# Low-rank products of an RWKV-style block packed three to the array, decay's by token halves, and the pieces of a step in a new order

## The reference

```python
xa = ln(x);  sx = shifted(xa) - xa
xxx = tanh((xa + sx * maa_x) @ maa_w1)              # 512 -> 5 streams x 32
xxx = einsum('blfd,fde->blfe', xxx, maa_w2)         # each stream 32 -> 512
xm = xa + sx * (maa_stack + xxx)                    # xk, xw, xv, xr, xg
w = exp(-exp(time_decay + tanh(xw @ td_w1) @ td_w2))  # 512 -> 64 -> 512
r, k, v = xr @ Wr.T, xk @ Wk.T, xv @ Wv.T;  g = silu(xg @ Wg.T)
# per head (32 heads of 16): out = r . (u * k v^T + s);  s = k v^T + w * s, token by token
og = groupnorm(out);  x1 = x + (og * g) @ Wo.T
xc = ln(x1);  x = x1 + sigmoid(xr2 @ Wfr.T) * (relu(xk2 @ Wfk.T)**2 @ Wfv.T)
```

## Time and profile before

| | |
|---|---|
| median of 3 runs | 3876.71 us (3876.33 to 3880.83) |
| the profiled execution | 3876.33 us; its span 3874.6 us |
| busy in the span | PE 94%, DVE 72%, ACT 48%, POOL 3% |
| mean granted TensorE clock | 0.972 |
| chain that ended last | PE 85%, DVE 7%, issue 3%, ACT 3%, SP's queue 2%, DMA 1% |

### The profile page before, as it was taken

One profiled execution on the slowest core, in us unless ns is written; L12 is line 12 of the kernel. 1 busy time (PEld: TensorE's weight loads), 2 busy tenths in 40 slices (PEclk: granted clock), 3 DMA queues, 4 the chain that ended last, 5 costly groups with the idle time before them and its releaser, 6 DMA issues.

```text
span 3874.6 us, 80327 instructions
## 1 busy us (share of the span) xinstructions
PE 3644.6 (94%) x33648; PEld 2808.0 (72%) x33648; DVE 2770.9 (72%) x4009; ACT 1853.5 (48%) x2867; POOL 109.9 (3%) x204
## 2 busy tenths in 40 slices
PE   6899999999999999999999999966998998998898
PEld 4677777777777777777777777753785686686587
DVE  3788888878888888888878888742674665565465
ACT  1455555545555455555555555532453453354353
POOL 1000000000000000000000000000000000000000
PEclk9899999999999999999999999978999999999999
DMA  2122233322233222332233322213230240231221
GB/s 109 55 72 99 89 108 110 123 99 102 95 108 110 93 96 99 123 108 101 88 110 110 110 100 95 100 62 112 50 99 22 57 111 13 66 76 48 66 46 44
DMA packets 90229, 337.19 MB, mean 87 GB/s; under 512 B 16512, under 2 KB 37632, under 8 KB 63360
## 3 DMA queue, kind: packets, MB, share of 16 engines
q0 software_dynamic: 27648, 201.34, 14.6%
q1 hardware_dynamic: 62208, 130.52, 11.7%
HBM read 252.11 MB, written 16.78 MB: 69 GB/s over the span
## 4 chain that ended last, share of the span: by engine, by line
PE 85%; DVE 7%; issue 3%; ACT 3%; SPq 2%; DMA 1%; POOL 0%; ACTq 0%; DVEq 0%; POOLq 0%
PE psum L663 33%; PE psum L949 9%; PE psum L672 5%; PE psum L732 4%; PE psum L895 3%; PE psum L960 3%; PE psum L709 3%; PE psum L924 3%; PE psum L633 3%; PE psum L936 2%; DVE rw L1482 2%; PE psum L897 1%; PE psum L979 1%; DVE psum L1664 1%; PE psum L644 1%
## 5 line engine op out<-in xcount | busy, mean ns | idle before, releaser
L663 PE MATMUL psum<-rw 128*128 128x256 f32 x6144 | 1426.7, 388 | 12.1 <-DVE rw L1320 7.2
L663 PEld LDWEIGHTS psum<-rw 128*128 128x128 f32 x6144 | 1173.0, 194 | 244.9 <-issue 76.0
L949 PEld LDWEIGHTS psum<-mem 128*128 128x128 f32 x4096 | 490.5, 192 | 27.2 <-issue 12.1
L949 PE MATMUL psum<-mem 128*128 128x128 f32 x4096 | 503.1, 276 | 0.0
L1278 ACT ACTIVATE mem<-psum,mem 128x1024 f32<-128x1024 f32 x256 | 285.4, 1115 | 435.4 <-DVE mem L1667 435.4
L1482 DVE TENSOR_TENSOR rw<-rw 128x2048 f32<-128x2048 f32 x192 | 432.7, 2285 | 11.9 <-PE psum L732 11.1
L1664 DVE CUSTOM_DVE_ANT_0 psum<-psum,mem 128x1024 f32<-128x1024 f32 x256 | 314.9, 1230 | 8.2 <-PE psum L936 6.6
L1365 DVE SCALAR_TENSOR_TENSOR rw<-psum,rw 128x256 f32<-128x256 f32 x480 | 199.2, 477 | 150.2 <-PE psum L633 94.0
L1675 DVE COPY mem<-psum 128x512 f32<-128x512 f32 x256 | 177.1, 692 | 133.7 <-PE psum L949 133.6
L1068 ACT ACTIVATE rw<-psum 128x512 f32<-128x512 f32 x192 | 111.8, 595 | 325.5 <-PE psum L663 325.3
L1106 ACT ACTIVATE rw<-psum 128x512 f32<-128x512 f32 x192 | 202.2, 1138 | 130.9 <-PE psum L709 129.2
(11 more groups left out here) (144 smaller groups left out, 4548.7 us busy)
## 6 DMA issues: line engine op xcount, KB each, us to landing
rw<-big_dram POOLq DMA_DIRECT2D x192, 1024.0 KB, 5.2
side<-mem SPq DMA_DIRECT2D x256, 128.0 KB, 2.3
rw<-xs_dram SPq DMA_DIRECT2D x32, 512.0 KB, 3.4
side<-mem SPq DMA_DIRECT2D x256, 64.0 KB, 2.0
rw<-rw SPq DMA_DIRECT2D x192, 64.0 KB, 3.1
xs_dram<-rw SPq DMA_DIRECT2D x24, 512.0 KB, 2.7
rw<-x_dram SPq DMA_DIRECT2D x16, 512.0 KB, 3.6
mem<-ctx_dram SPq DMA_DIRECT2D x4, 2048.0 KB, 9.3
```

The source lines that it names most:

```text
L663: last = mm(t[:, o * TC:(o + 1) * TC], big[:, k, P * m:P * m + P], src[:, k, 0:TC], start=k == 0, stop=k == KT - 1, skip_group_check=True)
L949: last = mm(t[:, P * o:P * o + P], probs[u % 2][:, h, P * st:P * st + P], diag[:, h, :], start=True, stop=True, skip_group_check=True)
```

## The change

1. The rows of the joint weight w2 now hold w, v, k, r (32 rows each); g takes k's place beside them. `lora_three` (L627) does w, v and k side by side in three row groups: two calls of six products. `lora_two` (L637, L638) does r, in rows 96 to 127, beside g, in rows 0 to 31: two calls of four products. `lora_pair` and `lora_k` are gone. The tiles in the ring become w2w0, w2v0, w2k0, w2w1, w2v1, w2k1, each call of `lora_three` taking all three banks.
2. `decay_in` (L651) computes each half of the tokens in its own 64 columns: eight products of 128 moving columns in place of four of 256, two side by side. The tanh then works on 128 partitions x 128. `decay_out` (L661) takes the token halves from the two row groups: eight products of 128 moving columns, two side by side, each half to its own bank. ACT empties these with eight instructions of 128 columns where four of 256 did.
3. `mixing` on DVE is cut in parts: the products of half 0 of w, v, k; those of half 1; then each stream's addition (`mixed`) as a piece of its own.
4. The pieces of the step stand in a new order on PE, DVE and ACT, with the orders of tiles and semaphore steps to match; k comes before r in weights and projections, and both fr tiles before both fk tiles.

```diff
-ROWS_OF = {"w": 0, "v": 1, "r": 2, "g": 3}
+ROWS_OF = {"w": 0, "v": 1, "k": 2, "r": 3}
...
-A_TILES = [("s1", "act"), ("m1", "dve"), ("s2", "act"), ("i1", "dve"), ("w1", "act"), ("w2w0", "dve"), ("w2v0", "dve"), ("w2w1", "dve"),
+A_TILES = [("s1", "act"), ("m1", "dve"), ("s2", "act"), ("i1", "dve"), ("w1", "act"), ("w2w0", "dve"), ("w2v0", "dve"), ("w2k0", "dve"),
...
-            def lora_k(it):
-                for n in range(2):
-                    t = opened(a_ring, it, f"w2k{n}")
-                    for o in range(2):
-                        m = 2 * n + o
-                        last = mm(t[:, o * TC:(o + 1) * TC], w2k[0:DM, P * m:P * m + P], thk[0:DM, :], start=True, stop=True, skip_group_check=True)
-                    a_ring.fill(last, it, f"w2k{n}")
-
-            def lora_pair(it, one, two, n):
-
-                pe.wait_ge(*a_ring.empty_at(it, "w1"))
-                t = [opened(a_ring, it, f"w2{s}{n}") for s in (one, two)]
+            def lora_three(it, n):
+
+                if n == 0:
+                    pe.wait_ge(*a_ring.empty_at(it, "w1"))
+                t = [opened(a_ring, it, f"w2{s}{n}") for s in "wvk"]
                 for o in range(2):
                     m = 2 * n + o
-                    for i, s in enumerate((one, two)):
+                    for i, s in enumerate("wvk"):
                         rows = slice(DM * ROWS_OF[s], DM * ROWS_OF[s] + DM)
...
+            def lora_two(it, n):
+
+                rows = slice(DM * ROWS_OF["r"], DM * ROWS_OF["r"] + DM)
+                t_r, t_g = opened(a_ring, it, f"w2r{n}"), opened(a_ring, it, f"w2g{n}")
+                for o in range(2):
+                    m = 2 * n + o
+                    last_r = mm(t_r[:, o * TC:(o + 1) * TC], w2[rows, P * m:P * m + P], th[rows, :], start=True, stop=True, skip_group_check=True)
+                    last_g = mm(t_g[:, o * TC:(o + 1) * TC], w2g[0:DM, P * m:P * m + P], thg[0:DM, :], start=True, stop=True, skip_group_check=True)
+                a_ring.fill(last_r, it, f"w2r{n}")
+                a_ring.fill(last_g, it, f"w2g{n}")
...
             def decay_in(it):
...
                 for k in range(KT):
-                    last = mm(t[0:DD, 0:TC], td1[:, k, :], mixed(it, "w")[:, k, :], start=k == 0, stop=k == KT - 1)
+                    for h in range(2):
+                        last = mm(t[DD * h:DD * h + DD, 0:P], td1[:, k, :], tokens(mixed(it, "w")[:, k, :], h), start=k == 0, stop=k == KT - 1, skip_group_check=True)
...
             def decay_out(it):
...
-                for n in range(2):
-                    t = opened(a_ring, it, f"td2_{n}")
-                    for o in range(2):
-                        m = 2 * n + o
-                        last = mm(t[:, o * TC:(o + 1) * TC], td2[0:DD, P * m:P * m + P], tdh[0:DD, :], start=True, stop=True, skip_group_check=True)
-                    a_ring.fill(last, it, f"td2_{n}")
+                t = [opened(a_ring, it, f"td2_{h}") for h in range(2)]
+                for m in range(KT):
+                    for h in range(2):
+                        rows = slice(DD * h, DD * h + DD)
+                        last = mm(t[h][:, P * m:P * m + P], td2[rows, P * m:P * m + P], tdh[rows, 0:P], start=True, stop=True, skip_group_check=True)
...
-                for n in range(2):
-                    t = filled(a_ring, it, f"td2_{n}")
-                    for o in range(2):
-                        last = f(hm["w"][:, 2 * n + o, :], t[:, o * TC:(o + 1) * TC], ACT.Exp, bias=par(layer, TDEC, 2 * n + o))
+                for h in range(2):
+                    t = filled(a_ring, it, f"td2_{h}")
+                    for m in range(KT):
+                        last = f(tokens(hm["w"][:, m, :], h), t[:, P * m:P * m + P], ACT.Exp, bias=par(layer, TDEC, m))
```

More of the change, by code:

```diff
@@ L763, in _ @@
                     feed(e, "fr", 0)
[L764 to L766 removed]
+                    feed(e, "fr", 1)
                 if 0 < n and has_n:
@@ L784, in _ @@
                 if has_b:
+                    products(b, "P2a")
                     products(b, "P2b")
+                if has_e:
+                    feed(e, "fk", 1)
+                if 0 < n and has_n:
+                    norm_a(n, "i1")
                 if has_c:
@@ L803, in _ @@
                 if has_b:
+                    products(b, "P4c")
+                    products(b, "P4d")
                     updates(b, 0, 0)
-                    products(b, "P4d")
                 if has_n:
-                    lora_pair(n, "w", "v", 0)
+                    lora_three(n, 0)
+                if has_b:
+                    updates(b, 0, 1)
+                    updates(b, 0, 2)
                 if has_c:
                     norm_c(c, "s1")
+                if has_n:
+                    lora_three(n, 1)
                 if has_b:
-                    updates(b, 0, 1)
-                if has_n:
-                    lora_pair(n, "w", "v", 1)
-                if has_b:
-                    updates(b, 0, 2)
                     updates(b, 0, 3)
@@ L849, in _ @@
                 if has_n:
+                    stream(n, "k", 0)
                     stream(n, "k", 1)
+                if has_b:
+                    own_outputs(b, 1)
+                if has_n:
+                    stream(n, "r", 0)
+                if has_b:
+                    outputs(b, 2, 0)
                 if has_c:
@@ L1174, in _ @@
                     norm_a(n, "s2")
+                if has_e:
+                    feed(e, "fk", 0)
+                    feed(e, "fk", 1)
+                if 0 < n and has_n:
                     norm_a(n, "xa")
@@ L1347, in norm_c, with mixing @@
                     c_dve.inc(mixture(mixk, sxc, xa_c, lambda k: par(layer, FMK, k)), it, "mixk")
[L1349 removed]
+            def mixing(it, streams, n):
                 layer = layer_of(it)
[L1351 to L1370 removed]
@@ new lines, in mixing @@
+                if n == 0:
+                    for s in streams:
+                        turn = STREAMS * it + ORDER.index(s)
+                        if turn >= 3:
+                            old_it, old = (turn - 3) // STREAMS, ORDER[(turn - 3) % STREAMS]
+                            dve.wait_ge(a_ring.full, a_ring.full_at(old_it, "td1" if old == "w" else old + "1"))
+                        if it and ORDER.index(s) < 3:
+                            dve.wait_ge(b_ring.full, b_ring.full_at(it - 1, "P4d"))
@@ new lines, in mixing, with mixed @@
+                for s in streams:
+                    t = filled(a_ring, it, f"w2{s}{n}")
+                    to = mix[(STREAMS * it + ORDER.index(s)) % 3]
+                    for o in range(2):
+                        m = 2 * n + o
+                        last = stt(to[:, m, :], t[:, o * TC:(o + 1) * TC], par(layer, MAAS, KT * FAN[s] + m), sxa[:, m, :], ALU.add, ALU.mult)
+                    a_ring.empty(last, it, f"w2{s}{n}")
+            def mixed(it, s):
+                to = mix[(STREAMS * it + ORDER.index(s)) % 3]
+                dve.wait_ge(*a_ring.empty_at(it, f"w2{s}1"))
+                a_dve.inc(tt(to, to, xa_a[:, :, PAD:PAD + TC], ALU.add), it, "mix_" + s)
@@ L1535, in _ @@
                     own_values(b)
+                if 0 < n and has_n:
+                    norm_a(n, "m1")
+                if has_b:
                     level2(b)
                     values(b, "P1", 0, 1, 0)
+                    level4(b)
+                if 0 < n and has_n:
+                    norm_a(n, "rc")
+                if has_b:
                     gather(b, "P1", "o1", 0, 1)
@@ L1577, in _ @@
                 if has_n:
-                    mixing(n, ("k",))
+                    mixed(n, "k")
                 if has_b:
```

221 lines of the change are left out of this document (98 added, 123 removed).

## The result

The changed kernel takes 3970.65 us (median of 4 runs, 3964.17 to 3986.08) against 3877.05 for the kernel before: ratio 1.0245, interval 1.0222 to 1.0267. Forecast was 3816, range 3780 to 3858. It is slower by 94 us where it should have been faster by 61.

What follows compares the result with a forecast made beforehand. PE bounds the whole steps, busy 102.78 of 103.00 us. 21 steps x 2.2 us = 46, clock 12, steps before and after 3: 61 us from 3876.33 gives 3816 us, range 3780 to 3858.

Steps and rivals of the forecast that it cites:

- The packing: On PE, lora_three and lora_two calls at 1.07 us, decay_in 1.04, decay_out 1.08: 3.59 us less a step.
- The rule of the Trainium skill: At decay_in: weight loads overlap running products only in different row groups, so column halves sharing rows would save nothing.
- Rival C: Row groups do not go three abreast and decay_out gains nothing: 2.0 us a step, 3859 us; chance 0.06.
- The new order: On PE, six groups of updates in place of five (+0.5) and P4d's lost place (-0.2): +0.3 us a step.
- the wait at `lora_three`: PE waits about 0.5 us at the second call for DVE to empty three banks; bounds 0.2 to 0.8.
- The wait at U10: PE's updates there wait for v_m's copies, 1.0 us late; 0.6 us taken together with lora_two's wait for ACT.
- The clock: PE's clock falls cost 21.8 us in all; 11.6 counted as gone, 10.2 left, 12 us gained in the sum.
- the second kind: Clock falls after stream k's and decay's products, some 3.3 us each; their 11.6 us counted as gone.
- Rival D: Chain mixing, scan, unit_out, store, v_m falls behind at U10; 5.0 us of waits a step, 3898 us; chance 0.06.
- Rival B: Emptying becomes the limit: 2.4 us of waits a step in place of 1.1, 3843 us; chance 0.20.
- A's time: Rival with no new wait and every fall of the clock gone: 3782 us; chance 0.20.
- The steps before the whole ones: Together with those after, where PE waits anyway and its work counts little: 3 us gained (0 to 6).

Runs made afterwards that it cites:

- u1: x1 with decay's products and exponentials taken back to four of 256 columns; 3838.40 us, 0.9897 of the kernel before.
- x2: The changed kernel with the load of g's weights held until v_m's pair 1 has landed; 3864.42 us, 0.9956 of the kernel before.
- x4: The kernel before with only decay's products by token halves, no packing of three and no new order; 3837.89 us, ratio 0.9895.
- x1: The changed kernel with v_m's pair 1 copies ahead of the store of x and load of x1 in SP's queue; 3795.61 us, 0.9779 of the kernel before.
- y2: x1 with a wait at U10 for DVE's emptying of w2g0, 2.1 us a step; 3970.51 us, 1.0240 of the kernel before.
- y1: x1 with a wait at U10 for a later DVE result (b10), 4.3 us a step; 4062.73 us, 1.0480 of the kernel before.
- z1: x1 with update group U03 moved ahead of lora_three's second call; 3799.24 us, 0.9798 of the kernel before.
- v1: x1 with projection fv0 moved behind lora_three's first call, its reader on DVE to match; 3779.27 us, 0.9747 of the kernel before.
- y3: x1 with a wait for the second scan ahead of stream k's projections, 4.1 us a step; 3941.37 us, 1.0167 of the kernel before.

## Why the prediction was wrong

By its own steps:

- **The packing, -3.59 a step: right.** 1.07, 1.02 and 1.09 us stand against the 1.07, 1.04 and 1.08 of the text; u1 shows decay's part in the step (1.68 for 1.67). The rule of the Trainium skill weighed there (TensorE: Matmul & The Clock Gate, Part 3), as the text worked it out, would have had `decay_in` gain nothing; the two column halves of the same rows ran side by side (1.02 us where the four products of 256 columns took 1.87), so the measurement decides against it for this case. Rival C falls with it.
- **The new order, +0.3, and the wait at `lora_three`, 0.5: right.** A step without a fall and without U10's wait is 100.0; the sum gives 100.1. The wait is 0.65.
- **The wait at U10, "bounds 0 and 1.0 (2 if the landing is slow)": this is the step that failed.** In the change it is 4.0 us on average in 15 steps of 21, 6.7 at most. The chain's first links were right (where no fall comes first, PE is ready for U10 12.8 us after `decay_in`'s start, 13.2 forecast; the store goes out 5.9 us after it, 6.1 forecast; the copies' first issue is 3.1 later, 3.05 forecast). Wrong was the last, taken from the earlier trace rows as if the landing time belonged to the copies: 5.0 us from the first issue to the last landing were counted, and it was 6.4 to 9.6 with a weight load issued among them. With that load held back (x2) it was 3.8 to 5.6. I had looked at the weights only for their own lateness ("the load of the next slot is hidden") and not at what runs beside them. x2 and the six steps without the wait show it.
- **The clock: a fall was counted as going or staying, never as caused by a new wait. This is the second step that failed.** Of the old falls the text was nearly right: the second kind went (x4), and x1 has 30.7 us of low clock where 20.4 were left in the sum. But no wait had a price beyond its own length, and the change has a fall in every one of the 21 steps. At U10 the fall costs more than the wait: y2 and y1 pay 8.0 and 11.9 us for 2.1 and 4.3. This is the larger half of the error: 6.3 of the step's 9.2 us over 100.0. The Trainium skill's rule in the text (same page, Part 1: the clock falls after idle) was used only to doubt a gain of 12 us, not for what a wait at U10 might bring; y1 and y2 have a fall that starts in or right behind the idle time in every step. It is not the whole rule either: z1 keeps its falls without the wait, and the earlier trace rows has falls with PE fully busy.
- **Rival D** named the right place and the right chain at 0.06, with 5.0 us of waits a step for 3898. The waits were 3.4 (both kinds, over 21 steps) and the time 3971, since D had no clock in it either, and "it decides from 4.0 us" was wrong: y2 is slower than before with 2.1 at U10, 2.7 of both kinds. Rival B's limit, the emptying of banks, costs 0.65 and no more; A's time (3782) is met by v1, with another order.
- **The steps before the whole ones, 3: too small.** They gave 22; PE is busy there for 91.53 of 95 us from 190 on (before 87.39 of the same stretch), at clock 0.98 for 0.93. The text had "their work counts little", but the order and the clock count there. How the 22 divide between them is not shown.

x1, which has no wait at U10, is 20 us below the forecast of 3816, its profiled execution (3800.92) 15; 11 of these are this last term (its first whole step starts at 269.6 for 283.5, 13.8 where 3 were counted).

## What to carry to other kernels

When an order is changed on one engine, list which large transfers it starts and when, and see what small transfer someone waits for at that time; a landing time read from a trace holds only beside the traffic it was read in. A wait of PE is priced by what follows it: ahead of full projections 4.1 us cost 6.8, ahead of small products 2.1 us cost 8.0, so a chain with less slack than its own spread must not end there. Issue what is already ready ahead of what is not in an in-order queue, and put a full-tile product between stretches of small ones.

## What was not expected of the hardware

- The lower clock lasts while PE is fully busy with small tiles: 14.30 of 14.30 us at 0.50 in y1, 14.90 of 14.90 in the change; with full tiles behind the wait the mean of the next 9.9 us is 0.83 (y3). With one full-tile projection moved in among the small ones there is no fall in 2104 us of the profiled execution (v1). Which property of the products it is, rows, columns or loads, stays open.
- Four copies of 64 KB within the chip take 3.8 to 4.9 us from the first issue in the whole steps before, where no weight load is issued among them (up to 5.6 in x2), and 6.4 to 9.6 us in the change with a 1 MB load among them, in a window with the DMA engines 79% busy at 272 GB/s.
- This was forecast, the second part against the rule weighed above: three row groups cost what two did (12 records in 1.07 us, 8 in 1.07), and two column halves of the same rows run side by side (16 records of 128 columns in 1.02 us).
